# A decoder layer in fp32: values by sixteen products in the keys' bank, y turned a group ahead, and the last groups' bias by TensorE

## What is computed

```
x = layernorm(x + (linear attention with its own norm, then a 128-512-128 MLP with table gelu))
x = layernorm(x + cross_attention(x, ctx, mask))
x = layernorm(x + ffn(x))

cross_attention: q = x WQ; k = ctx WK; v = ctx WV        # 16 heads of 8 features
    scores = q k^T / sqrt(8); masked and future keys get -1e9
    out = softmax(scores) v WO
ffn: p = softmax(x W_gate)                               # 7 gates
    w = p_top1 / (p_top1 + p_top2) and p_top2 / (...)    # both go to the same expert matrix
    out = x W_shared^T + (sum of w) * (x W_expert^T) + bias
```

## Time and profile before

| | |
|---|---|
| median of 3 runs | 563.21 us (560.77, 563.21, 564.78) |
| the profiled execution's own time | 561.41 us |
| its span, first to last instruction | 559.7 us |
| TensorE products busy | 491.0 us (88%) |
| VectorE busy | 404.7 us (72%) |
| GpSimd busy | 374.7 us (67%) |
| ScalarE busy | 363.9 us (65%) |
| mean granted TensorE clock | 0.973 |

### The profile page before, as it was taken

One profiled execution on the slowest core, in us unless ns is written; L12 is line 12 of the kernel. 1 busy time (PEld: TensorE's weight loads), 2 busy tenths in 40 slices (PEclk: granted clock), 3 DMA queues, 4 the chain that ended last, 5 costly groups with the idle time before them and its releaser, 6 DMA issues. The chain is left out here.

```text
span 559.7 us, 22010 instructions
## 1 busy us (share of the span) xinstructions
PE 491.0 (88%) x8800; PEld 365.4 (65%) x8800; DVE 404.7 (72%) x1406; ACT 363.9 (65%) x685; POOL 374.7 (67%) x686
## 2 busy tenths in 40 slices
PE   2899999998999999997899999899998999998750
PEld 1777777775777767774567667676676666766530
DVE  2677777755777776556678878688887888888764
ACT  1566666555777777747777677677677676777432
POOL 6566666645577774833337878778787887879553
PEclk9999999999999999999999999899999999999775
DMA  6530000000000000002000111111201121010001
GB/s 167 169 117 2 3 2 1 4 2 1 2 0 3 1 1 1 2 7 49 17 23 4 50 51 26 28 50 50 49 6 49 51 50 50 5 51 21 22 2 57
DMA packets 24742, 17.38 MB, mean 31 GB/s; under 512 B 2112, under 2 KB 22464, under 8 KB 24640
## 3 DMA queue, kind: packets, MB, share of 16 engines
q1 hardware_dynamic: 24208, 15.90, 10.7%
q10 hardware_dynamic: 432, 0.07, 0.1%
HBM read 11.77 MB, written 4.19 MB: 29 GB/s over the span
## 5 line engine op out<-in xcount | busy, mean ns | idle before, releaser
L783 ACT ACTIVATE gel<-gel,row_scale 128x512 f32<-128x512 f32 x96 | 66.1, 720 | 29.2 <-DVE gel L1056 19.0
L790 ACT ACTIVATE gel<-pair 128x1024 f32<-128x1024 f32 x64 | 51.8, 809 | 29.0 <-PE pair L1414 28.5
L1354 PEld LDWEIGHTS pair<-w,gel 128*128 128x128 f32 x512 | 60.4, 192 | 8.0 <-issue 5.7
L1043 DVE TENSOR_REDUCE neg_max<-pair 128x16 f32<-128x1024 f32 x64 | 60.5, 945 | 5.1 <-PE pair L1368 5.0
L1354 PE MATMUL pair<-w,gel 128*128 128x128 f32 x512 | 62.4, 276 | 1.0 <-ACT gel L715 1.0
L1318 PE MATMUL pair<-hT,w 128*128 128x512 f32 x128 | 58.3, 596 | 1.3 <-ACT lev L710 1.3
L1414 PE MATMUL pair<-ident,gel 128*128 128x128 f32 x384 | 55.7, 280 | 2.9 <-ACT gel L783 1.9
L532 POOL TENSOR_SCALAR k_exp<-k_sb,quad_mask 128x512 f32<-128x512 f32 x64 | 43.0, 690 | 20.8 <-ACT k_sb L762 12.7
L1414 PEld LDWEIGHTS pair<-ident,gel 128*128 128x128 f32 x384 | 43.4, 141 | 19.1 <-issue 13.5
L1368 PE MATMUL pair<-k_exp,qT 32*32 32x128 f32 (+1 forms) x2048 | 44.5, 333 | 2.6 <-issue 2.4
L509 POOL TENSOR_TENSOR X<-X,proj_sb 128x512 f32<-128x512 f32 x16 | 20.3, 1270 | 35.6 <-ACT proj_sb L673 35.6
(11 more groups left out here) (138 smaller groups left out, 1221.9 us busy)
## 6 DMA issues: line engine op xcount, KB each, us to landing
X<-in_x SPq DMA_DIRECT2D x16, 256.0 KB, 3.1
cT<-in_ctx SPq DMA_DIRECT2D x16, 256.0 KB, 3.9
out_rows<-X SPq DMA_DIRECT2D x15, 256.0 KB, 2.4
mask_rows<-in_mask_early SPq DMA_DIRECT2D x16, 128.0 KB, 3.6
w<-in_L_attn_w SPq DMA_DIRECT2D x2, 256.0 KB, 3.4
out_rows<-X SPq DMA_DIRECT2D x2, 128.0 KB, 1.8
w_kv<-in_L_attn_wk SPq DMA_DIRECT2D x1, 64.0 KB, 3.3
w_q<-in_L_attn_wq ACTq DMA_DIRECT2D x1, 64.0 KB, 3.1
```

Of the source, the lines that this page charges most:

```text
L783: nc.scalar.activation(part, part, ACT.Exp, scale=row_scale[:, n:n + 1])\
L790: nc.scalar.activation(pT[par].rearrange("p (a c) -> p a c", a=2), turned, ACT.Copy)\
L1043: nc.vector.tensor_reduce(neg_max[par][:, :].rearrange("p (a h) -> p a h", a=2), scores, AX.X, ALU.max, negate=True).then_inc(max_ready, 1)
L1354: last = nc.tensor.matmul(bank(6 + q)[:, P * t:P * (t + 1)], gel[:, q, f, P * t:P * (t + 1)], w_2[:, f, :], start=(f == 0), stop=(f == NF ...
```

## The change

The value projection, `project_v`, makes sixteen products of 64 tokens by 64 features instead of four of 128 by 128, so that even and odd heads land on their own half of the partitions, in bank 5 instead of bank 4. `copy_v` then needs two instructions instead of four. The turning of y and its copy move from slot 0 of the step that projects q from it to slot 3 of the step before. MOE_BANK becomes 6, 4, 5, 5, with the waits that follow. In the end, TensorE adds the bias for groups 14 and 15 by a product of the identity with the bias into the same bank; VectorE mixes group 14; GpSimd makes the rows of group 13 instead of ScalarE. Only what repeats these points is cut.

```diff
-MOE_BANK = [5, 6, 4, 5]
+MOE_BANK = [6, 4, 5, 5]
...
 # GpSimd, end()
                 ln_deviation(pool, ln_b, k1, mv_b, veps_b, rstd_b[0], second)
-                mixture(LAST - 1, q)
-                end_offset(LAST - 2, rstd_c, offs_b[0])
+                last_norm(LAST - 2, LAST % 2)
                 end_offset(LAST - 1, rstd_b[1], offs_b[1])
-                add_bias(LAST, 2)
                 pool.wait_ge(ln_c.done, LAST - 1)
                 ln_deviation(pool, ln_c, LAST, mv_c, veps_c, rstd_c)
...
 # ScalarE, copy_v(g, q)
-                values = bank(first_bank(g, 4)).rearrange("p (u h i e) -> p u h i e", u=TG, h=2, e=DH)
-                for b in range(2):
-                    for h in range(2):
-                        batches = v2[q][h * S:(h + 1) * S, :, :, h, 0:DH] \
-                            .rearrange("p (u b) i e -> p u b i e", b=2)
-                        last = nc.scalar.activation(batches[:, :, b, :, :],
-                                                    values[b * S:(b + 1) * S, :, h, :, :], ACT.Copy)
+                for h in range(2):
+                    rows = slice(h * S, (h + 1) * S)
+                    last = nc.scalar.activation(
+                        v2[q][rows, :, :, h, 0:DH],
+                        bank(first_bank(g, 5))[rows, :].rearrange("p (b i e) -> p b i e", i=HH, e=DH),
+                        ACT.Copy)
...
 # ScalarE, phase3
-                    if t == 0 and exists(s - 2):
-                        collect((s - 2) * TG + TG - 1, TG - 1, p)
+                    if s == 0 and t == 0:
+                        copy_y(1)
                     if t == 0 and exists(prev):
                         act.wait_ge(xatt_xposed, prev + 1)
                         after(act, xproj_done, prev)
                         nc.scalar.activation(attT[:, :], bank(6), ACT.Copy).then_inc(xattT_ready, 1)
-                    if t == 0 and exists(nxt):
-                        copy_y(nxt)
+                    if t == 0 and exists(s - 2):
+                        collect((s - 2) * TG + TG - 1, TG - 1, p)
                     if t == TG - 1 and exists(prev):
                         ...
                         nc.scalar.activation(y2T[:, :], bank(6), ACT.Copy).then_inc(y2T_ready, 1)
+                    if t == TG - 1 and exists(s + 2):
+                        copy_y(s + 2)
...
 # ScalarE, end(): one collection ahead of the attended copy instead of two, and
-                end_rows(LAST - 2, p, rstd_c, offs_b[0])
                 end_rows(LAST - 1, q, rstd_b[1], offs_b[1])
...
 # VectorE, end()
                 gate_weights(LAST - 1)
+                mixture(LAST - 1, q)
                 gate_top(LAST, 2)
+                last_statistics(LAST - 1, q)
                 gate_weights(LAST)
-                last_statistics(LAST - 1, q)
                 mixture(LAST, 2)
...
 # TensorE, project_v(g, q)
-                for u in range(TG):
-                    last = nc.tensor.matmul(bank(first_bank(g, 4))[:, P * u:P * (u + 1)],
-                                            cT[q][:, P * u:P * (u + 1)], w_xv[:, :], start=True, stop=True)
+                for u in range(2 * TG):
+                    for h in range(2):
+                        last = nc.tensor.matmul(bank(first_bank(g, 5))[h * S:(h + 1) * S,
+                                                                       FH * u:FH * (u + 1)],
+                                                cT[q][:, S * u:S * (u + 1)],
+                                                w_xv[:, FH * h:FH * (h + 1)],
+                                                start=True, stop=True)
...
+            def moe_biased(g, t):
+                nc.tensor.matmul(bank(t)[:, 0:2 * D + NE], y2T[:, P * t:P * (t + 1)], w_moe[:, :],
+                                 start=True, stop=False)
+                nc.tensor.matmul(bank(t)[:, 0:D], ident[:, :], bias_bc[:, :], start=False, stop=True)\
                     .then_inc(moe_done, 1)
...
 # TensorE, phase3
-                    if t == 0 and exists(s - 2):
-                        pe.wait_ge(moe_ready, (s - 2) * TG + 1)
-                        moe(s - 2, TG - 1)
+                    if n == 0:
+                        turn_y(1)
                     if t == 0 and exists(r):
                         pe.wait_ge(xatt_ready, r * TG + TG)
-                        after(pe, moe_ready, (s - 1) * TG - 2)
+                        after(pe, moe_ready, (s - 1) * TG - 3)
                         turn_attended(q, 6, range(TG))
-                    if t == 0 and exists(g):
-                        after(pe, moe_ready, (s - 1) * TG - 1)
-                        after(pe, v2_ready, g)
-                        turn_y(g)
+                    if t == 0 and exists(s - 2):
+                        pe.wait_ge(moe_ready, (s - 2) * TG + 3)
+                        moe(s - 2, TG - 1)
...
                     if t == 1 and exists(g):
                         pe.wait_ge(yT_ready, g + 1)
+                        after(pe, moe_ready, (s - 1) * TG - 2)
                         project_qk(yT, w_xq, bank(4), xq_done)
                     if t == 2 and exists(g):
+                        pe.wait_ge(k_ready, g + 1)
+                        project_v(g, q)
+                    if t == 3 and exists(s + 2):
                         pe.wait_ge(q_ready, g + 1)
-                        project_v(g, q)
+                        turn_y(s + 2)
...
                     if t == 3 and exists(r) and s < LAST:
                         pe.wait_ge(y2T_ready, r + 1)
-                        if exists(g):
-                            pe.wait_ge(k_ready, g + 1)
                         for u in range(TG - 1):
+                            if u == 1 and exists(g):
+                                pe.wait_ge(yT_ready, min(s + 3, NG))
                             if u == 2 and exists(g):
                                 pe.wait_ge(v2_ready, g + 1)
                             moe(r, u)
...
 # TensorE, end(): moe(LAST - 1, u, u) and moe(LAST, u, u) become moe_biased, and
-                for u in range(2):
-                    moe(LAST - 1, u, u)
+                moe_biased(LAST - 1, 0)
                 pe.wait_ge(xatt_ready, NT)
                 pe.wait_ge(xattT_ready, NG)
                 turn_attended(p, 4, second)
-                moe(LAST - 1, 2, 2)
+                moe_biased(LAST - 1, 1)
                 ...
                 rows_product(bank(5), attT, w_xo[:, :], second).then_inc(xproj_done, 1)
-                moe(LAST - 1, 3, 3)
+                moe_biased(LAST - 1, 2)
+                moe_biased(LAST - 1, 3)
```

More of the change, by code:

```diff
@@ L609, in end_offset @@
                 ln_deviation(pool, ln_c, g, mv_c, veps_c, rstd)
+                pool.wait_ge(ln_c.done, g)
                 nc.gpsimd.tensor_tensor(negm_c[:, :], mv_c[:, :, 0], minus_one[:, :], ALU.mult)\
@@ L846, in end_rows @@
             def end_rows(g, q, rstd, offs):
-                act.wait_ge(end_offs, g - LAST + 3)
+                act.wait_ge(end_offs, 1)
                 for t in range(TG):
@@ L853, in end @@
             def end():
-                p, q = LAST % 2, 1 - LAST % 2
+                q = 1 - LAST % 2
                 (k0, first), (k1, second) = halves
-                for u in range(2):
-                    collect((LAST - 1) * TG + u, u, q, u)
+                collect((LAST - 1) * TG, 0, q, 0)
                 act.wait_ge(xatt_xposed, NG + 1)
                 copy_half(4, attT, second)
-                for u in range(2, TG):
+                for u in range(1, TG):
                     collect((LAST - 1) * TG + u, u, q, u)
@@ L1095, in mixture @@
             def mixture(g, p):
-                dve.wait_ge(bias_ready, g + 1)
+                if g == LAST - 2:
+                    dve.wait_ge(bias_ready, g + 1)
                 for t in range(TG):
@@ L1457, in project_v, with moe @@
             def project_v(g, q):
-                for u in range(TG):
-                    last = nc.tensor.matmul(bank(first_bank(g, 4))[:, P * u:P * (u + 1)],
-                                            cT[q][:, P * u:P * (u + 1)], w_xv[:, :], start=True, stop=True)
+                for u in range(2 * TG):
[5 more added lines that the diff above has]
+                                                start=True, stop=True)
                 last.then_inc(xv_done, 1)
-            def moe(g, t, dst=None):
-                nc.tensor.matmul(bank(MOE_BANK[t] if dst is None else dst)[:, 0:2 * D + NE],
+            def moe(g, t):
+                nc.tensor.matmul(bank(MOE_BANK[t])[:, 0:2 * D + NE],
                                  y2T[:, P * t:P * (t + 1)], w_moe[:, :], start=True, stop=True)\
+                    .then_inc(moe_done, 1)
+            def moe_biased(g, t):
+                nc.tensor.matmul(bank(t)[:, 0:2 * D + NE], y2T[:, P * t:P * (t + 1)], w_moe[:, :],
+                                 start=True, stop=False)
+                nc.tensor.matmul(bank(t)[:, 0:D], ident[:, :], bias_bc[:, :], start=False, stop=True)\
```

(2 more changed lines are left out.)

## The result

The changed kernel takes 557.7 us (median of 20 runs, 554.28 to 562.99), the kernel before 562.45 in the runs beside it (20 runs, 557.8 to 565.42). The ratio is 0.9922 with a 95% interval of 0.9897 to 0.9946, so 4.4 us faster, between 3.0 and 5.8. One of the changed kernel's runs, 562.99 us, counts as slow and is left out of the ratio. A second set of 10 runs gave 0.9912 [0.9883, 0.9941]. Forecast were 559.2 us and a change of -4.0.

The account below looks back on a forecast made before the run. GpSimd's loop of 17.25 us was taken to set the usual step, and a chain the end. The end's -4.3 and early steps' +0.3 gave 557.4 from 561.41 us; with 1.8 added for the median, 559.2, range 555.5 to 564.5.

Parts of the forecast that it names:

- What bounds the step: Usual step: GpSimd's loop of 17.25 us, 15.4 of work and 1.87 of round trip to VectorE; TensorE's loop is 16.86.
- Value products: TensorE ahead of slot 2's scores: sixteen products take 1.06 us as the four did, nothing added; even 2.1 would be covered.
- the rival in which the passes take turns: Slot 2: column halves do not run side by side, slower; most weight near 573 us, up to 591; chance 0.07.
- The copy in two: ScalarE's copy of the values falls from 1.61 us to 1.2; the 0.4 us less is worth nothing.
- y a group ahead: y's transposes move from slot 0 to slot 3: TensorE's loop grows to about 16.96 us, hidden by GpSimd's 17.25; early steps +0.3.
- slot 3 pays in full: Rival: y's turns and ScalarE's copy come on top in slot 3, loop 17.5 us, 562.7 us in all; chance 0.14.
- The end: Tail chain in four terms: last scaling starts at 552.0 instead of 556.31, -4.3 us, of which 1.26 is the bias itself.
- the end gives half: Rival: bias products at half clock throughout, VectorE's mixture and GpSimd's rows in each other's way: 561.2 us; chance 0.12.
- the first two terms: End, ahead of the last maxima: earlier scalings against eight bias products on TensorE, taken as 0; VectorE's mixture, taken as nothing.
- the second term: End: group 14's mixture, 1.14 us, goes to VectorE into its 1.37 us idle ahead of 543.75 and costs nothing.
- The sum: End -4.3 us and early steps +0.3 make -4.0 us.
- More than the sum: Rival: the clock stays up in the end (-1.4 us) and the pauses, 3.4 us together, mostly vanish: 555 us; chance 0.16.

Follow-up runs that it names:

- experiments 5 and 9: Kernel before with the new end; 5 leaves out GpSimd's bias of groups 0 to 12 (552.65 us), 9 moves the steps' bias to VectorE (553.57 us).
- experiment 2: The changed kernel's steps (sixteen value products, y turned in slot 3) with the end of the kernel before: 560.23 us, ratio 0.9986.
- experiment 6: The changed kernel with GpSimd's bias of groups 0 to 12 left out: 553.55 us, ratio 0.9825.
- experiment 7: Kernel before with only the end's bias of groups 14 and 15 by TensorE; GpSimd still mixes group 14, ScalarE scales group 13's rows: 557.59 us.
- end-only kernel: Steps and MOE_BANK of the kernel before with the changed kernel's end: 554.65 us, ratio 0.9889; run again, 556.54 us, 0.9908.

## Why the prediction was right

**What bounds the step** was right and is shown: with GpSimd relieved, the steps without a pause fell from 17.25 to 16.86 us (experiments 5 and 9).

**Value products:** 1.15 us instead of 1.06, and covered by slot 2's idle time, as argued; the rival in which the passes take turns (66 ns or more) fell with 36 ns. The rule weighed against this step, by the Trainium skill's "TensorE: Matmul & The Clock Gate", section on packing small matmuls, that a weight load overlaps running products only when its row group differs, did not come true here. The estimate made from it was 80 ns a pass, and the trace has 36 ns for passes that use all rows and half of the columns.

**The copy in two** was right in size (0.34 us, 0.4 forecast) and wrong in worth. I read GpSimd's values' copy as following its rows directly, though 0.10 lay between them; with earlier values GpSimd's loop is 17.12 instead of 17.25. Over twelve steps that is 1.6 us which the forecast did not have. No time of a run shows it by itself: experiment 2 has the changed steps at 0.8 us less than before, between 2.6 less and 1.0 more, and the forecast of 0.3 more lies in that too.

**y a group ahead:** TensorE's loop became 16.95 to 16.96, forecast 16.96, and stayed under GpSimd's. The rival "slot 3 pays in full" (17.5) is refuted by the steps of experiment 6. The early steps' +0.3 is too small to be seen beside the pauses.

**The end:** the stretch from the maxima to the last scaling gave -4.35 against -4.3, and that its rest is GpSimd's queue is shown by experiment 7. The rival "the end gives half" fell. The stretch ahead of the maxima was right in its sum and not in its parts. At the same full clock it is 23.88 against 23.8 to 24.0, so the 0 taken for the first two terms holds. But beside experiment 2, the turns come 0.92 us earlier (20.34 behind the attended copy instead of 21.26), the bias products and what follows give back 0.28, and the last expert products are collected 0.64 us earlier. VectorE then comes late by nearly as much: its mixture, for which the second term took nothing, stands right ahead of the maxima, which start 0.6 us after the last collection and not 0.1.

```profile
544.83 1.14 DVE L1098 SCALAR_TENSOR_TENSOR moe_out<-moe_out,top_sum 128x128 f32<-128x128 f32 x4
...
544.88 0.39 ACT L796 ACTIVATE moe_out<-pair 128x263 f32<-128x263 f32 x1 [0.28 <-PE pair L1477]
```

In experiment 7, where GpSimd keeps that mixture, the maxima follow the collection after 0.1 us. So two misses of about 0.6 and 0.5 us cancel, and the 0 was partly luck. The working gave it for a half clock, and the last products of the changed kernel ran at the full one.

**The sum:** -4.0 forecast, -4.4 [-5.8, -3.0] measured. The level, 559.2 against 557.7, is off by 1.5 us; half of it is the median of before, which moved from 563.21 (3 runs) to 562.45 (20 runs).

**More than the sum** has a true part: the clock in the end differs from one execution to the next. From the attended copy to the last maxima it is 25.72 us before and 25.24 in experiment 7, both with the clock at 0.50 from 529 to 532 us, and 23.4 to 24.3 in all others. The long stretch at 0.50 does not explain this alone, for two of the others have it too (24.27 and 24.32). Pauses that vanish were the rival's other part, and they did not.

What remains open is what makes TensorE pause. They come near the same instants in different kernels (286, 303, 355 and 427 us with sixteen products; 285, 357 and 428 in the end-only kernel), so they may belong to places in the list of instructions; their lengths differ between executions. No experiment here took their cause away. Why the clock falls behind some of them and not behind others of the same length is open as well. The clock goes with the time over the runs of one kernel: of 66 runs of before beside the experiments, the 16 with a mean clock of 0.979 take 560.6 us on the mean, and the 9 with 0.967 take 565.1. That is as much as the whole gain of the change, so it is the clock that one has to look at first when two single executions are compared.

## What to carry to other kernels

An engine that is busy for 93% of a step need not be the one that sets the step: compare two steps of different length, and see which engine's loop has the length of each. In a tail, look for the small operation that a result waits for behind unrelated work on its engine; its place in the queue cost nearly twice its own time here. One profile of each kernel can put several microseconds in the wrong stage when pauses and clock differ from one execution to the next; kernels with one part of the change, each run several times, tell them apart. A forecast that comes true in its sum should still be compared term by term: here two terms were off and cancelled.

## What the runs showed of the hardware

Two column halves of the array worked side by side with all rows in use: a pass with 64 columns of weights and 64 streamed took 36 ns, one of 128 and 128 took 133, and halves that take turns would have needed 66. The clock fell to 0.50 behind 14 of the pauses of TensorE of 1.1 to 2.2 us, and each such step cost about 3 us instead of 1 to 2. An fp32 scaling on VectorE, two at 0.60 us together, took 1.46 beside one TENSOR_TENSOR of GpSimd in every profile that had both; the lock of the shared port in the Trainium skill's "SBUF — State Buffer", section "Who interferes with whom", would do that, and the trace agrees. Moving that GpSimd operation was worth 0.86 us to VectorE, which does not wait for its result there.
